# Moving half of the output projection's matmuls from the output loop into the scan loop

## The reference

```
h   = layernorm(x)
xin, z = split(h @ W_in)                     # 2 x 2048 channels
xc  = silu(causal_conv4(xin))
dt_in, B, C = split(xc @ W_x)                # 1024, 16, 16
dt  = softplus(dt_in @ W_dt + b_dt)
for each channel i and state s:              # scan over the 2048 rows
    state = exp(dt * A[i, s]) * state + dt * B[s] * xc
    y    += state * C[s]
yg  = (y + xc) * silu(z)
x   = x + layernorm(yg @ W_out)              # the "mix"
x   = x + layernorm(layernorm(x) @ W[idx] + b[idx])
```

## Time and profile before

| | us |
|---|---|
| median of 3 runs | 4912.14 (4908.43 to 4914.44) |
| profiled execution, its own time | 4913.57 |
| its span, slowest core (core 7) | 4911.9 |
| spans of the 8 cores | 4891.7 to 4911.9 |
| busy: VectorE | 2964.7 (60%) |
| busy: TensorE, matmuls | 1744.9 (36%) |
| busy: ScalarE | 1089.1 (22%) |
| mean granted TensorE clock | 0.539 |

### The profile page before, as it was taken

The page is one execution under the profiler, slowest core; times in us unless marked ns, Lnnn a source line. Parts: engine busy times, 40 slices in busy tenths (PEclk is TensorE's granted clock), DMA queues, the critical chain, the costliest instruction groups (busy, mean ns, idle before and its releaser), DMA issues.

```text
span 4911.9 us, 21290 instructions; the slowest of 8 cores (4891.7 to 4911.9 us)
## 1 busy us (share of the span) xinstructions
PE 1744.9 (36%) x3461; PEld 346.9 (7%) x3461; DVE 2964.7 (60%) x3227; ACT 1089.1 (22%) x1550; POOL 110.8 (2%) x201
## 2 busy tenths in 40 slices
PE   2775870011003444333388201010010102566564
PEld 0221110000000000000011000000000000111110
DVE  3220018878887677777400788888888883343334
ACT  2220132222222222222112322222222220000100
POOL 0111000000000000000000000000000000000000
PEclk9996555555555555555555555555555555555555
DMA  2663000000001111111200101000000002000000
GB/s 57 120 128 68 0 5 13 13 24 15 17 17 24 28 30 26 26 26 26 56 0 5 26 13 26 13 15 11 9 17 9 13 6 92 17 26 23 21 26 22
DMA packets 64531, 136.11 MB, mean 28 GB/s; under 512 B 7726, under 2 KB 7854, under 8 KB 64278
## 3 DMA queue, kind: packets, MB, share of 16 engines
q0 software_dynamic: 28080, 52.74, 7.2%
q1 hardware_dynamic: 36326, 82.02, 5.1%
HBM read 149.70 MB, written 35.65 MB: 38 GB/s over the span
## 4 chain that ended last, share of the span: by engine, by line
DVE 51%; PE 24%; issue 11%; DMA 6%; ACT 6%; SPq 1%; DVEq 1%; POOL 0%; ACTq 0%; POOLq 0%
DVE big_b L736 12%; DVE big_b L722 11%; DVE big_b L744 6%; DVE sm L715 6%; PE psB L932 3%; PE psA L932 3%; DVE bigf L772 2%; PE psE L597 2%; PE psA L597 2%; DMA sm<-d_sz 2%; PE psB L597 2%; PE psE L438 2%; DVE big_b L758 2%; DVE big_b L763 2%; PE psB L438 2%
## 5 line engine op out<-in xcount | busy, mean ns | idle before, releaser
L709 ACT ACTIVATE bigf<-bigf,pa 128x1024 f32<-128x1024 f32 x512 | 584.4, 1147 | 1755.9 <-DVE big_b L736 839.5
L722 DVE TENSOR_TENSOR_SCAN big_b<-bigf,sm 128x1024 bf16<-128x1024 f32 x256 | 586.6, 2292 | 129.4 <-ACT bigf L709 87.0
L736 DVE TENSOR_TENSOR_SCAN big_b<-bigf,hcol,sm 128x1024 bf16<-128x1024 f32 x256 | 601.9, 2351 | 45.4 <-DVE sm L715 42.7
L686 DVE TENSOR_TENSOR bigf<-bigf 128x512 f32<-128x512 f32 x64 | 41.4, 685 | 632.7 <-ACT bigf L680 632.7
L744 DVE TENSOR_TENSOR big_b<-big_b,big_a 128x1024 bf16<-128x1024 bf16 x512 | 351.7, 687 | 28.6 <-DVE big_b L736 1.8
L715 DVE TENSOR_TENSOR sm<-sm,big_a 128x1024 bf16<-128x1024 bf16 x512 | 350.6, 685 | 1.8 <-DVE sm L692 0.2
L438 PE MATMUL psB<-arena,big_b 128*128 128x512 bf16 x344 | 168.4, 490 | 227.7 <-ACT bigf L669 107.2
L408 PE MATMUL psT<-big_b 128*128 128x128 bf16 x32 | 8.5, 266 | 671.7 <-DVE big_b L401 663.4
L438 PE MATMUL psA<-arena,big_b 128*128 128x512 bf16 x336 | 165.5, 492 | 227.6 <-ACT bigf L669 158.3
L655 PE MATMUL psE<-arena,big_b 128*128 128x512 bf16 x168 | 98.8, 588 | 396.6 <-ACT bigf L669 374.6
L655 PE MATMUL psA<-arena,big_b 128*128 128x512 bf16 x168 | 98.7, 588 | 377.3 <-ACT bigf L669 355.3
(11 more groups left out here) (158 smaller groups left out, 2325.7 us busy)
## 6 DMA issues: line engine op xcount, KB each, us to landing
big_b<-w_in POOLq DMA_DIRECT2D x64, 256.0 KB, 4.4
sm<-ffn_w POOLq DMA_DIRECT2D x64, 256.0 KB, 6.1
convh<-x SPq DMA_DIRECT2D x16, 512.0 KB, 3.6
big_b<-w_dt POOLq DMA_DIRECT2D x32, 256.0 KB, 4.1
sm<-d_xconv SPq DMA_DIRECT2D x32, 256.0 KB, 3.4
sm<-d_sz SPq DMA_DIRECT2D x32, 256.0 KB, 4.0
d_yg<-big_b SPq DMA_DIRECT2D x32, 256.0 KB, 2.5
big_a<-d_yg SPq DMA_DIRECT2D x16, 512.0 KB
```

The costliest lines, as they stand in the source:

```text
L709: return e.activation(bigf[:, T1 + sp * 1024:T1 + (sp + 1) * 1024], bigf[:, DTB:DTB + 1024], AF.Exp, scale=pa[:, it * 16 + s:it * 16 + s + 1])
L722: return e.tensor_tensor_scan(big_b[:, HLn:HLn + 1024], bigf[:, T1 + sp * 1024:T1 + (sp + 1) * 1024], sm[:, 6144:7168], 0.0, ALU.mult, ALU ...
L736: return e.tensor_tensor_scan(big_b[:, HLn:HLn + 1024], bigf[:, T1 + sp * 1024:T1 + (sp + 1) * 1024], sm[:, 6144:7168], hcol[:, ic:ic + 1] ...
```

## The change

Half of the mixes, those of row tiles 0 to 7 that need only the first half's results, are computed in passes 8 to 15 of the second scan loop. A new function `emit_mix_early(lt)` loads the 16 blocks of 128 channels by 128 rows from `d_yg` into one of four parts of the upper half of `arena`, does the 32 matmuls into psC and psD, has ScalarE copy them as bf16 to `big_b` columns 16384 to 17408, and stores these to a new DRAM buffer `d_mix`. In the output loop `emit_mix(lt)` for `lt` below 8 is now one DMA on GpSimd's queue, from `d_mix` (bf16) to the float32 buffer. Before the output loop only the second half's columns of `d_yg` are loaded: 16 DMAs of 256 KB. Nothing else is changed.

```diff
+    d_mix = nc.dram_tensor("d_mix", [8, 128, D], BF16, kind="Internal").ap()
...
+        def emit_mix_early(lt):
+            ab = 8192 + (lt % 4) * 2048
+            for it in range(NT):
+                def f_ly(e, lt=lt, it=it, ab=ab):
+                    return e.dma_start(
+                        out=arena[:, ab + it * 128:ab + (it + 1) * 128],
+                        in_=d_yg[it][:, lt * 128:(lt + 1) * 128])
+                kb.op("sync", f_ly, kind="dma", r=[("d_yg", it * 2, it * 2 + 1)],
+                      w=[("arena", ab + it * 128, ab + (it + 1) * 128)])
+            for n2 in range(2):
+                ps, pk = (psC, "psC") if n2 == 0 else (psD, "psD")
+                for it in range(NT):
+                    def f_mm(e, n2=n2, it=it, ps=ps, ab=ab):
+                        return e.matmul(
+                            ps[:, 0:512],
+                            arena[:, ab + it * 128:ab + (it + 1) * 128],
+                            big_b[:, it * 1024 + n2 * 512:it * 1024 + n2 * 512 + 512],
+                            start=(it == 0), stop=(it == 15))
+                    kb.op("tensor", f_mm,
+                          r=[("arena", ab, ab + 2048), ("big_b", 0, 16384)], w=[pk])
+                def f_ev(e, n2=n2, ps=ps):
+                    return e.copy(big_b[:, 16384 + n2 * 512:16384 + n2 * 512 + 512],
+                                  ps[:, 0:512])
+                kb.op("scalar", f_ev, r=[pk],
+                      w=[("big_b", 16384 + n2 * 512, 16384 + n2 * 512 + 512)])
+            def f_sp(e, lt=lt):
+                return e.dma_start(out=d_mix[lt], in_=big_b[:, 16384:17408])
+            kb.op("sync", f_sp, kind="dma", r=[("big_b", 16384, 17408)],
+                  w=[("d_mix", lt, lt + 1)])
...
+            else:
+                emit_mix_early(it - 8)
...
-                return e.dma_start(out=big_a[:, it * L:(it + 1) * L], in_=d_yg[it])
+                return e.dma_start(out=big_a[:, it * L + 1024:(it + 1) * L],
+                                   in_=d_yg[it][:, 1024:2048])
...
         def emit_mix(lt):
             mb = T2 + (lt % 2) * 1024
+            if lt < 8:
+                def f_lm(e, lt=lt, mb=mb):
+                    return e.dma_start(out=bigf[:, mb:mb + 1024], in_=d_mix[lt])
+                kb.op("gpsimd", f_lm, kind="dma", r=[("d_mix", lt, lt + 1)],
+                      w=[("bigf", mb, mb + 1024)])
+                return
```

More of the change, by code:

```diff
@@ L833, in build_nc @@
                           w=[("big_b", k * 1024, (k + 1) * 1024)])
+            else:
+                emit_mix_early(it - 8)
         for it in range(NT):
             def f_lyg(e, it=it):
-                return e.dma_start(out=big_a[:, it * L:(it + 1) * L], in_=d_yg[it])
-            kb.op("sync", f_lyg, kind="dma", r=[("d_yg", it * 2, it * 2 + 2)],
-                  w=[("big_a", it * L, (it + 1) * L)])
+                return e.dma_start(out=big_a[:, it * L + 1024:(it + 1) * L],
+                                   in_=d_yg[it][:, 1024:2048])
+            kb.op("sync", f_lyg, kind="dma", r=[("d_yg", it * 2 + 1, it * 2 + 2)],
+                  w=[("big_a", it * L + 1024, (it + 1) * L)])
         kb.op("gpsimd", lambda e: e.dma_start(out=sm[:, 0:7168], in_=d_weff[:, 0:7168]),
```

## The result

The changed kernel takes 5047.79 us (median of 8 runs, 5039.23 to 5050.92) against 4913.69 us for the kernel before (8 runs, 4908.43 to 4925.05): ratio 1.0268, 95% interval 1.0257 to 1.0279. The forecast was 5046 us, 5013 to 5105.

What follows compares the result with a forecast made beforehand. The prediction took VectorE to bound the scan stage and the mix to gate output loop periods. Scan stalls +213.5, output loop start -28.2 and six shorter periods -51.1 gave +134 us: 5046 us, range 5013 to 5105.

Steps and rivals of the forecast that it cites:

- What bounds each stage: Scan stage goes at VectorE's pace; in the output loop the mix gates the period, costing 8.51 us, not 23.15.
- The queues: Scan passes: small loads stand behind the pass's result store on SP; next exponentials behind the copies, next scan behind the store.
- The stall: Second scan loop: each added mix followed by a pass delays the scan 30.5 us; seven make 213.5 us.
- the sum: Whole kernel: +213.5 - 28.2 - 51.1 = +134 us, giving 5046 us.
- The sign given for it: Changed profile, passes 9 to 15: VectorE idle 35 to 40 us before the first scan, ended by a DMA.
- The output loop: Six periods from tile 0 to tile 6 shorten by 8.51 us each, saving 51.1 us; converting loads cost nothing.
- The start of the output loop: Between last scan pass and first norm: norm at 4152.0 instead of 4180.23, 28.2 us earlier.
- Full clock in the added mixes: Early mixes: 32 matmuls take 16.2 us instead of 23.15, saving 56 us in eight: 4990 us; chance 0.05.
- Slow small loads: Early mixes: loads make each of eight mixes 7 us longer, 5102 us; held as the forecast's upper part, no separate chance.
- the 15.2 us that the prediction had estimated for sixteen blocks: Early mixes' small loads, one after the other at the skill page's 0.95 us: some 8 us more per mix, about 62 in all.
- The output loop's gain: Rival: output loop periods stay at 47.07 us through the converting load or a shared semaphore, 5097 us; chance 0.06.
- The rival on the other side: Scan passes: small loads run ahead on SP, added work free in passes 8 to 14, 4833 us; chance 0.04.

Runs made afterwards that it cites:

- e1_ahead: Changed kernel with each early mix's loads and matmuls emitted before the pass in which they run, copies and store still behind it: 4835.11 us, 0.9849 to the kernel before.
- e7_late_out: Changed kernel with early mixes' copies and store in columns of their own, emitted inside the next pass before state 12 (mix 7's stay): 4831.59 us, ratio 0.9848.
- e10_weights_later: Changed kernel with GpSimd's 2 MB load of the linear weights held back until mix 7 has been stored: 5037.74 us, 1.0267 to the kernel before.
- e2_own_columns: Changed kernel with only the columns of the early copies and store moved to unused big_b columns from 25088: 5036.00 us, 1.0257 to the kernel before.
- e6_one_load: Changed kernel with the 16 small loads of each early mix made one 512 KB DMA: 5009.17 us, 1.0205 to the kernel before.

## Why the prediction was right

**What bounds each stage** held. The added matmuls cost by the wait of VectorE, 206 us, and the removed ones were worth what TensorE held up, not their busy time.

**The queues.** SP's loads went out behind the pass's store, and the next scan stood behind ScalarE's copies and the store. e1_ahead and e7_late_out show it from both sides: one emits the loads a pass earlier, the other the copies and the store 12 states later, and each turns the loss into a gain. What both change is the distance between the matmuls and what waits for them. One sentence of the prediction went too far: that for the step to cost nothing the loads would have to land before the pass ends. In e7_late_out they land after it, and the passes take 86.0 us.

**The stall**, forecast at 30.5 us, was 29.5. Small loads, in the pass shown: 16 issues in 7.40 us where 7.5 was taken, matmuls 8.8 us after the first where 9.6 was (8.8 to 9.6 in the seven passes). Matmuls: 23.1 us as forecast. Store to scan: 2.1 us where 2.6 was taken. Seven stalls were 206.3 us, 7 less than the sum had. The sign given for it, 35 to 40 us of idle VectorE before the scan, mixed up two lengths: some 36 us is the time from the pass to the scan, and VectorE works in a part of it.

**The output loop** saved 6 x 47.07 - 229.2 = 53.2 us in six periods, 2 more than forecast, as a short period was 38.2 us and not 38.56. Mixes 8 to 15 gated eight periods at 47.1 us, and the converting load (L964) was never waited for.

**The start of the output loop** was the worst term: 18.2 us saved on the slowest core instead of 28.2. The bias work began 62.2 us after the pass and not 52. Of the 10 us, 7.4 lie in the small loads of mix 7: matmuls 17.8 us after the first issue, where 4098 - 4087.66 = 10.3 was taken. That 2 MB of weights lie beside them had been seen and priced at under 1 us; e10_weights_later shows that they cost 8.7 on the slowest cores, and 5.5 on six of the eight. Another 2.5 us lie in the big loads, 19.5 us to the bias work instead of 17. On those six cores this term saved 23 us (68 against 91.4, the middle of the eight before) and missed by 5.

So the sum, 134 against 135, is better than its terms: -7 and -2 us stand against +10 us. That they meet so closely is luck. On the mean of the eight cores the spans grew by 130.7 us (4904.4 to 5035.0), and the slowest core was one of the two with the slow start.

**The rivals.** Full clock in the added mixes did not come: 0.50 in all eight of them, 0.73 us from matmul to matmul. Slow small loads did not come either, but for mix 7; nor did the 15.2 us that the prediction had estimated for sixteen blocks. The output loop's gain was whole. The rival on the other side, loads that run ahead, needed another program: e1_ahead is that program. That its 4835 us meet the rival's 4833 is partly luck: the shared count adds 29 us in the passes, and the first norm comes 51 us sooner than before the change where the rival had 28. That the shared columns alone are worth little, 1.5 us a pass, held in e2_own_columns with 1.0; that they are worth 4 us once the rest is hidden had not been thought of.

## What to carry to other kernels

Work moved into a stage where its engine is idle is free only if no engine that sets the pace has anything behind it in a queue, a buffer or a shared semaphore count; look at what the added instructions wait for and then at who stands behind each. Issue loads whose data is long there ahead of the instruction that waits for the end of the pass, or let the copies be emitted only where their result is already due: in e1_ahead the first took the stall away but for the 3.9 us of the shared count, in e7_late_out the second did, with columns of their own. When a wait is taken away, expect the next one in line to bear nearly the same price, as the store and the exponentials did here; remove the cause that both share. Before a term is read off the slowest core, look at the same stretch on the others: the start of the output loop was 7 us longer on one core than on six.

## What the runs showed of the hardware

Sixteen loads of 32 KB with rows of 256 B took 8.8 to 9.6 us from the first issue until TensorE could start, the same 512 KB as one load 5.6 to 6.3 us (e6_one_load). Beside 2 MB of weights on GpSimd's queue the sixteen took 14.5 to 17.8 us, by core, and 9.0 to 9.2 with the weights moved behind them (e10_weights_later). So sixteen DMAs instead of one cost 3.1 us here, and the traffic beside them 5.5 to 8.7, by core; 512 KB in 5.7 us is 92 GB/s, landing included. The Trainium skill, "DMA: Bandwidth & Descriptors" (Specifications), says that rows under 512 B stay below line rate. The runs do not speak against it, as 16 loads of 2 KB rows moved 4 MB in 16.6 us, 253 GB/s, but these are also eight times the bytes, and no run here moves the same bytes in longer rows.

The granted clock was 0.50 in the scan stage and in the added matmuls, the level of 1.2 GHz, and a matmul of 512 columns with weights of its own started every 0.73 us there.
